# The mixture's hidden product in another order: silu in place in its PSUM bank, the gates' rows before the up product

## What is computed

```python
g = jnp.einsum('th,eih->eti', x, expert_gate)
u = jnp.einsum('th,eih->eti', x, expert_up)
outs = jnp.einsum('eti,ehi->eth', jax.nn.silu(g) * u, expert_down)
outs_t = jnp.transpose(outs, (1, 0, 2))
gathered = jnp.take_along_axis(outs_t, topk_idx[:, :, None], axis=1)
final = (gathered * topk_w[:, :, None]).sum(1)
```

## Time and profile before

| | us |
|---|---|
| median of 3 runs | 569.41 (568.24 to 569.56) |
| the profiled execution, whole | 567.0 |
| its span, first to last instruction | 565.3 |
| PE busy | 512.8 |
| DVE busy | 476.3 |
| POOL busy | 382.8 |
| ACT busy | 293.7 |
| mean granted TensorE clock | 0.968 |

### The profile page before, as it was taken

How to read it: one execution, slowest core, us unless ns; L and a number is a source line. 1 busy time by engine, 2 the same in 40 slices (tenths; PEclk the granted TensorE clock), 3 DMA queues, 4 the chain that set the end, 5 groups by cost and what they waited for, 6 DMA issues and landing times.

```text
span 565.3 us, 8827 instructions
## 1 busy us (share of the span) xinstructions
PE 512.8 (91%) x2860; PEld 408.0 (72%) x2860; DVE 476.3 (84%) x866; ACT 293.7 (52%) x793; POOL 382.8 (68%) x329
## 2 busy tenths in 40 slices
PE   3999999999999998389899999999999999999765
PEld 3965776776676675278788788888888888887634
DVE  6946877976985778989998999999999999999946
ACT  3341352353244225345766767767667667668423
POOL 4960010031203657596899999999999999999971
PEclk9998999999999999869999999999999999999958
DMA  7442322233223231011011110111111110101002
GB/s 229 184 150 71 103 90 102 95 97 115 90 94 116 94 89 45 16 38 37 20 45 33 52 43 20 56 38 39 38 35 42 38 43 34 37 20 38 19 2 74
DMA packets 26674, 37.08 MB, mean 66 GB/s; under 512 B 4480, under 2 KB 12296, under 8 KB 26500
## 3 DMA queue, kind: packets, MB, share of 16 engines
q1 hardware_dynamic: 26628, 36.52, 20.9%
HBM read 25.75 MB, written 1.31 MB: 48 GB/s over the span
## 4 chain that ended last, share of the span: by engine, by line
PE 63%; ACT 18%; DVE 12%; issue 5%; DMA 1%; POOLq 0%; POOL 0%; ACTq 0%; DVEq 0%
PE bank L585 62%; ACT shared L1143 6%; ACT bank L1152 4%; ACT shared L1113 3%; ACT z_ln L1135 2%; DVE bank L1539 2%; PE bank L588 2%; DVE shared L1533 1%; DVE shared L1564 1%; DVE ln_stats L1225 1%; DVE shared L1368 1%; DVE shared L1241 1%; DVE z_ms L1553 1%; DMA x<-in_x 1%; DVE shared L1623 0%
## 5 line engine op out<-in xcount | busy, mean ns | idle before, releaser
L585 PE MATMUL bank<-w,shared 128*128 128x128 f32 x1024 | 122.8, 278 | 0.3
L585 PE MATMUL bank<-xnT_lo,wgu_hi 128*128 128x512 f32 x264 | 121.2, 459 | 0.4 <-ACT shared L1143 0.4
L585 PEld LDWEIGHTS bank<-w,shared 128*128 128x128 f32 x1024 | 116.7, 192 | 6.3 <-ACT shared L1143 6.2
L585 PE MATMUL bank<-xnT_hi,wgu_lo 128*128 128x512 f32 x264 | 106.3, 402 | 0.0
L585 PE MATMUL bank<-xnT_hi,wgu_hi 128*128 128x512 f32 x264 | 105.6, 400 | 0.0
L523 POOL TENSOR_TENSOR shared<-shared 128x1024 f32<-128x1024 f32 x36 | 86.0, 2389 | 13.0 <-DVE shared L1564 13.0
L585 PE MATMUL bank<-shared 128*128 128x512 f32 (+3 forms) x280 | 89.9, 445 | 0.0
L1013 ACT ACTIVATE shared<-bank 128x512 f32<-128x512 f32 x68 | 40.7, 598 | 88.4 <-PE bank L585 88.1
L1143 ACT ACTIVATE shared<-bank,b 128x512 f32<-128x512 f32 x128 | 82.0, 701 | 1.5 <-PE bank L585 1.5
L1539 DVE TENSOR_REDUCE bank<-shared 128x64 f32<-128x2048 f32 x36 | 82.4, 2288 | 0.3
L1564 DVE TENSOR_TENSOR shared<-shared,bank 128x2048 f32<-128x2048 f32 x36 | 82.0, 2278 | 0.1
(11 more groups left out here) (169 smaller groups left out, 778.7 us busy)
## 6 DMA issues: line engine op xcount, KB each, us to landing
shared<-gate_rows SPq DMA_DIRECT2D x122, 128.0 KB, 2.9
w<-in_w SPq DMA_DIRECT2D x8, 256.0 KB, 2.9
shared<-in_w SPq DMA_DIRECT2D x1, 2048.0 KB, 8.5
left_tok<-state_ext SPq DMA_DIRECT2D x16, 128.0 KB
left_tok<-state_ext SPq DMA_DIRECT2D x8, 224.0 KB
left_tok<-state_ext SPq DMA_DIRECT2D x8, 192.0 KB
shared<-in_wd SPq DMA_DIRECT2D x1, 1088.0 KB, 11.8
x<-in_x SPq DMA_DIRECT2D x4, 256.0 KB, 4.0
```

Source lines behind the costliest of these rows:

```text
L585: return nc.tensor.matmul(out, lhsT, rhs, start=start, stop=stop)
```

## The change

ACT writes silu back into the gate product's own bank instead of into `silu_g`. DVE multiplies that bank by the gates' rows first (new semaphore `gated_done`), then the result by the up product's bank, and that gives `h0`. PE's gate product of item `n` waits for `gated_done` of item `n - 2`, its up product for `h0_done` of item `n - 2`. The shared expert's items and the first three routed items (`n < RING`) stay as they were. ACT no longer waits for DVE before silu, since `silu_g` isn't written. At the seam three waits are put on the new semaphores.

```diff
@@ gate_up (PE)
-                for m, out, free in ((0, bank[G[i % 2]], "silu_done"), (1, bank[U[i % 2]], "gu_done")):
-                    after(pe, s(free), i - 1)
+                for m, out in ((0, bank[G[i % 2]]), (1, bank[U[i % 2]])):
+
+                    if i - 2 < item(RING):
+                        after(pe, s(("silu_done", "gu_done")[m]), i - 1)
+                    elif m == 0:
+                        pe.wait_ge(s("gated_done"), i - 1 - item(RING))
+                    else:
+                        pe.wait_ge(s("h0_done"), i - 1 - item(0))
@@ sum_channels, values (PE), left_out (ACT): the seam
-                    pe.wait_ge(s("silu_done"), item(B * PAIRS))
+                    pe.wait_ge(s("gated_done"), B * PAIRS - RING)
...
-                    pe.wait_ge(s("gu_done"), item(B * PAIRS))
+                    pe.wait_ge(s("h0_done"), B * PAIRS)
...
-            act.wait_ge(s("silu_done"), item(B * PAIRS))
+            act.wait_ge(s("gated_done"), B * PAIRS - RING)
@@ silu_gate (ACT)
-                after(act, s("gu_done"), i - 1)
-                a.activation(silu_g[:, i % 2], bank[G[i % 2]][:], ACT.Silu).then_inc(s("silu_done"), 1)
+                if i < item(RING):
+                    after(act, s("gu_done"), i - 1)
+
+                a.activation(silu_g[:, i % 2] if i < item(RING) else bank[G[i % 2]][:], bank[G[i % 2]][:], ACT.Silu).then_inc(s("silu_done"), 1)
@@ routed_hidden (DVE)
                 dve.wait_ge(s("silu_done"), i + 1)
+                if n < RING:
+                    dve.wait_ge(s("u_mm"), i + 1)
+                    tt(silu_gu[:, i % 2], silu_g[:, i % 2], bank[U[i % 2]][:], ALU.mult).then_inc(s("gu_done"), 1)
+                    dve.wait_ge(s("gu_done"), i + 1)
+                    dve.wait_ge(s("gb_mm"), n + 1)
+                    tt(h0[:, n % RING], silu_gu[:, i % 2], bank[GB][:], ALU.mult).then_inc(s("h0_done"), 1)
+                    return
+
+                dve.wait_ge(s(f"ld_rows{n % RING}"), 32 * (n // RING))
+                tt(silu_gu[:, i % 2], bank[G[i % 2]][:], gate_rows[n % RING], ALU.mult).then_inc(s("gated_done"), 1)
+                dve.wait_ge(s("gated_done"), n - RING + 1)
                 dve.wait_ge(s("u_mm"), i + 1)
-                tt(silu_gu[:, i % 2], silu_g[:, i % 2], bank[U[i % 2]][:], ALU.mult).then_inc(s("gu_done"), 1)
-                dve.wait_ge(s("gu_done"), i + 1)
-                if n < RING:
-                    dve.wait_ge(s("gb_mm"), n + 1)
-                else:
-                    dve.wait_ge(s(f"ld_rows{n % RING}"), 32 * (n // RING))
-                if n >= RING:
-                    dve.wait_ge(s("dn_mm"), downs(n - RING))
-                tt(h0[:, n % RING], silu_gu[:, i % 2], gate_rows[n % RING] if n >= RING else bank[GB][:], ALU.mult).then_inc(s("h0_done"), 1)
+                dve.wait_ge(s("dn_mm"), downs(n - RING))
+                tt(h0[:, n % RING], silu_gu[:, i % 2], bank[U[i % 2]][:], ALU.mult).then_inc(s("h0_done"), 1)
```

More of the change, by code:

```diff
@@ L273, in build @@
             "woc_done gram_mm gram_cp q_mm q_cp route0_step parts_done g0T_mm g0T_cp "
-            "g_mm u_mm gb_mm st_gates ld_rows0 ld_rows1 ld_rows2 silu_done gu_done h0_done dn_mm y0_silu y0T_mm sg_done x1_done "
+            "g_mm u_mm gb_mm st_gates ld_rows0 ld_rows1 ld_rows2 silu_done gu_done gated_done h0_done dn_mm y0_silu y0T_mm sg_done x1_done "
             "m1_mm m1_done st_mm st_done head_mul state_done stT_mm stT_cp so_mm so_cp at_mm at_cp at_stat at_var_done "
```

## The result

| | before | after |
|---|---|---|
| median of 19 runs each, us | 569.46 (566.13 to 571.28) | 566.07 (562.82 to 569.98) |
| mean of the same runs, us | 569.32 | 566.96 |
| ratio of the times | | 0.996 (0.9941 to 0.9979) |
| the profiled execution, whole / span, us | 567.0 / 565.3 | 569.98 / 568.3 |

By the means the changed kernel is faster by 0.4%; on 569.4 us the interval is 1.2 to 3.4 us. The medians lie 3.4 us apart, because after's runs fall into groups and its median is in a low one. The forecast was 568.8 us with a range down to 567.2.

A forecast was written before the change was run, and what follows sets the result against it. PE was taken to bound the mixture and POOL's queue its end (the seam). ACT, DVE, PE and rows 0, seam -0.6 us: from the median 569.41 to 568.8 us, range 567.2 to 570.2.

The forecast's parts named there:

- ACT 0: Mixture: silu into the bank differs by at most 0.05 us per item, hidden by PE's pace; taken as 0.
- DVE's products in the mixture 0, no long ones left: Mixture: both products read a bank and escape collisions with POOL, all at 0.69 us; 0 in the sum.
- PE and the rows 0: Mixture: banks held 0.69 us longer and gates' rows needed one product earlier, both covered by slack; 0.
- Nobody waits for it: Mixture: the first product no longer waits for the up product, h0 comes a tenth or two of a us earlier; 0.
- POOL decides, not DVE: Mixture's end: L1424 waits for PE's transposes, which wait for POOL's L509, so POOL's gain counts; 0.9 us upper end.
- the hand count: Mixture's end: stepping DVE and POOL forward, the scan's `products` (L1533) start about 1.7 us earlier.
- The seam, 0.6 us: Mixture's end, from 220 us: POOL gains 0.9 us, less 0.3 for router steps pushing in; 0.6 us faster.
- The clock, put at 0 in the sum: PE's granted clock: no term in the sum; a different clock appeared only in two rivals.
- Rival (a): Mixture's end: freed POOL instructions run into router steps, or the scan absorbs the gain; 569.4 us, chance 0.18.
- (d): Mixture: PE stalls because a bank is held too long, five stalls of 0.5 us; 571.9 us, chance 0.04.
- Rival (b): Behind the seam: PE keeps full clock through 16 matmuls, winning 1.2 us more; 567.6 us, chance 0.17.
- Rival (c): Scan's first expert matmuls: low clock lasts some 5 us longer, costing up to 2.5 us; 571.3 us, chance 0.06.

The follow-up runs named there:

- e1: Kernel before with only the order of DVE's two products changed, silu still going to SBUF: 569.92 us, ratio 1.0013.
- e3: Changed kernel with the last four items (60 to 63) put back in the old form: 567.97 us, ratio 0.9982.
- g1: Changed kernel with one more POOL subtraction of 1.27 us, result unused, ahead of the scan's first sum: 569.44 us, ratio 1.0012.
- g2: Kernel before with the scan's first sum and product on POOL moved earlier into POOL's idle time: 569.12 us, ratio 1.0007.
- e2: Kernel before with only the last four items (60 to 63) in the new form: 566.55 us, ratio 0.9961.
- f2: Changed kernel with unused filler matmuls in PE's idle times, at the seam and near the end: 565.31 us, ratio 0.9937.
- f3: Changed kernel with unused filler matmuls in PE's idle times at the seam alone: 569.12 us, ratio 1.0005.

## Why the prediction failed

- **ACT 0.** Right: silu into the bank 0.016 us cheaper, hidden.
- **DVE's products in the mixture 0, no long ones left.** Right: 61 at 0.69. The mechanism (two SBUF inputs collide with POOL) is confirmed by e1 and e3. The rule of the Trainium skill, "SBUF — State Buffer", section "SBUF: two separate sides", agrees for the products: none of after's 122 with a bank input took longer than 0.70 us, and the router's subtraction ended with POOL's L523. A second SBUF input is not the only case, though: the router's L1503 compares one SBUF tile with a constant and took 1.23 us beside POOL's L478, which had started 0.09 us ahead of it. In after the same step (L1515, at 221.74, 0.02 us behind L478's start) took 0.19, and L478 took 1.33. So which engine waits turns on a few hundredths of a us. The rule of "VectorE: DVE Perf Modes", section "Rules for kernel authors", to copy to SBUF first, finds nothing here: 0.692 (two in SBUF before), 0.687 (one in a bank after).
- **PE and the rows 0.** Right: PE 20.00 of 20, no wait for either product, and the offset to before doesn't change from 34 to 213 us. "Nobody waits for it", of the earlier first product, was not quite so: two of DVE's polar steps came 0.14 us sooner, and PE with them, but nothing of it reached the seam (0.49 at item 63, and e3).
- **"POOL decides, not DVE".** Right for the changed kernel: PE's transposes wait for L509, DVE waits 1.21 us for PE, and g1's POOL delay alone takes the gain back. For the kernel before it is only half right, since both chains ended within 0.1 us of each other, and g2 shows DVE's to be the next limit. The forecast came out of this unharmed because the change sped up DVE's chain more (2.56 us; the hand count had said 1.7).
- **The seam, 0.6 us.** This is the step that failed, in its size: 1.32 was measured. The upper end of 0.9 was the sum of L476 (0.46) and L509 (0.45), which came out at 0.45 and 0.44. Missing was a third collision, 0.50 at L451 and L457. I looked for long products only, and the product beside L457 was not long; I had no look at POOL's rows there. And the 0.3 taken off for router steps that push in was too much: 0.08 was lost. 0.50 + 0.45 + 0.44 - 0.08 is 1.31. I had forecast L1424 at about 229.7; it came at 228.48, or 228.94 with the start-up's 0.46 added back.
- **The clock, put at 0 in the sum.** The seam at its true size would have made the forecast 568.1 us, still inside the stated range and 2.0 above the median. The rest has no shown cause: the median of after is 0.9 below its own mean, and the other 1 us between the means is the part that stays open above.
- **Rival (a), nothing gained**, and **(d), banks stall PE**: did not happen.
- **Rival (b), the clock falls otherwise, 567.6.** Its mechanism was seen (1.95 us instead of 3.07) and brought nothing in this profile, since DVE's next router step then ended only with POOL's L523. Its price was wrong by the same thing as the seam's: a collision that wasn't looked for. **Rival (c)**, more low clock in the scan: the profiled run of after has it, at 2.6 us on the chain, near the 2.5 I gave it. That nearness is luck, since it is not the low stretch that (c) names. That one ended earlier than before's (249.3 against 253.1 us), and the 2.6 us come from another, from 269.8 to 276.6.
- **The range.** Its lower end was (b)'s 567.6 and the spread of three timed runs, 1.3 us. Nineteen runs of before spread over 5.2 us. With the seam at its true size and 1 to 2 us either way for the clock, the range would have had to reach to about 566. The chances for "faster" (0.17) rested on the same two faults.

## What to carry to other kernels

When a DVE instruction with two SBUF inputs goes away beside a busy POOL, go through POOL's rows and compare each with its own undisturbed length. The DVE instruction may look normal while POOL pays 0.5 us. Then ask who waits for POOL, and whether another chain ends at the same moment: the same change was worth nothing that could be told in 57 items where PE set the pace, and all of it in four items where POOL's and DVE's queues did. A kernel whose runs spread by 1% has to be measured by enough runs. Fillers in PE's idle times narrow that spread, but both kernels of the pair have to be profiled to see which low stretches are left.

## What the runs showed of the hardware

- POOL's L457 took 1.42 us alone and 1.77 to 1.91 beside a DVE product of 0.69 with two SBUF inputs; L451 took 3.13 alone, 3.25 in before and 3.67 in e1. The cast took 0.61 alone and 1.07 beside one. The loss is on either side: the other product, beside L462, took 1.69 and POOL's 1.29 was untouched. A small subtraction of 128 x 64 took 0.26 us or, under POOL's L523, 1.41. A comparison of one SBUF tile of 128 x 64 with a constant took 0.19 when it began 0.02 us behind POOL's subtraction (after), 1.29 at 0.04 us (e2) and 1.23 at 0.09 us (before).
- Silu of 128 x 512 took 0.582 us from a bank into the same bank, at each of after's 61 instructions, and 0.591 to 0.615 (median 0.598) into SBUF in before.
- Twenty filler matmuls at the end of the kernel (f2 against f3) took 3.8 us off the mean: the clock was low from 534.8 to 541.6 us instead of from 534.9 to 551.9. Thirty-two at the seam alone (f3) gave 569.12 us against after's 566.96. Its profiled run is low from 268.6 to 275.5, in a stretch where PE is on the chain, as after's and f2's are too, so whether the fillers bring that stretch is not shown.
